# Gated cross-attention and a routed feed-forward on one core: the two additions of a wide tile to the output, each half with a semaphore of its own

## The reference, cut to what matters

```
x = x + tanh(g_xattn) * cross_attention(ctx, layernorm(x))      # 16 x 256 tokens, width 256, 8 heads of 128
n = layernorm(x)
gates = (n @ Wg + bg) / 1.000001
weights, experts = top_k(gates, 2);  weights = softmax(weights)  # 8 experts
for each token:
    x += tanh(g_ffn) * sum over its 2 experts e of
         weight_e * (silu(n @ W1[e] + b1[e]) @ W2[e] + b2[e])    # hidden width 1024
```

## Time and profile before

| | us |
|---|---|
| median of 3 runs (lowest, highest) | 1546.25 (1545.76, 1546.97) |
| the profiled execution | 1545.36 |
| its span | 1543.7 |
| PE busy | 1502.7 |
| additions (L926, 71): time of the instructions on POOL | 119.9 |
| additions: idle time of POOL before them | 207.2 |

### The profile page before, as it was taken

The page is one execution under the profiler, slowest core; times in us unless marked ns, Lnnn a source line. Parts: engine busy times, 40 slices in busy tenths (PEclk is TensorE's granted clock), DMA queues, the critical chain, the costliest instruction groups (busy, mean ns, idle before and its releaser), DMA issues.

```text
span 1543.7 us, 29968 instructions
## 1 busy us (share of the span) xinstructions
PE 1502.7 (97%) x10446; PEld 1384.4 (90%) x10446; DVE 1114.2 (72%) x2692; ACT 949.8 (62%) x2057; POOL 596.2 (39%) x710
## 2 busy tenths in 40 slices
PE   8999999999999999999999999999999999999986
PEld 6889888898888889898888888888999999999976
DVE  7677777777777777777777777777767766666675
ACT  5555655556555655556556555556668777777765
POOL 5332424334342333423334342332444545444442
PEclk9999999999999999999999999999999999999999
DMA  4000100000000000000000000022546645544553
GB/s 164 4 21 8 22 8 22 28 8 22 8 22 7 22 29 8 22 8 22 29 1 29 8 22 8 8 79 67 121 136 192 162 128 137 150 127 127 150 145 82
DMA packets 57823, 91.13 MB, mean 59 GB/s; under 512 B 8617, under 2 KB 44774, under 8 KB 57550
## 3 DMA queue, kind: packets, MB, share of 16 engines
q1 hardware_dynamic: 41710, 70.19, 14.4%
q0 software_dynamic: 15824, 18.98, 6.6%
q10 hardware_dynamic: 144, 0.05, 0.0%
HBM read 70.91 MB, written 18.29 MB: 58 GB/s over the span
## 4 chain that ended last, share of the span: by engine, by line
PE 81%; DVE 9%; DMA 5%; ACT 2%; issue 2%; POOL 1%; ACTq 0%; DVEq 0%; POOLq 0%
PE ring L194 12%; PE ring L195 12%; PE ring L196 12%; PE turn L1269 6%; DMA out_rows<-yo,token 4%; PE ph L196 3%; PE score L194 3%; PE ph L194 3%; PE py L194 3%; PE py L196 3%; PE py L195 3%; PE ph L195 3%; PE score L196 3%; PE score L195 3%; PE proj L195 2%
## 5 line engine op out<-in xcount | busy, mean ns | idle before, releaser
L901 POOL TENSOR_SCALAR probs<-probs,rsum 128x512 f32<-128x512 f32 x256 | 174.2, 692 | 532.4 <-DVE rsum L1589 532.4
L1115 ACT ACTIVATE pt_hi<-turn 128x512 fp32r<-128x512 f32 x256 | 139.2, 595 | 238.5 <-PE turn L1269 238.5
L926 POOL DMA_INDIRECT out_rows<-yo,token x71 | 119.9, 1689 | 207.2 <-DMA out_rows<-yo,token 133.4
L1714 DVE TENSOR_TENSOR ht_lo<-hs,ht_hi 128x512 fp32r<-128x512 f32 x142 | 98.2, 691 | 120.9 <-ACT ht_hi L1082 117.5
L1583 DVE TENSOR_REDUCE smax<-score 128x1 f32<-128x512 f32 x256 | 169.7, 685 | 13.5 <-PE score L196 13.1
L1016 ACT ACTIVATE probs<-score,nbias 128x512 f32<-128x512 f32 x256 | 173.2, 686 | 3.6 <-DVE nbias L1585 3.6
L1073 ACT ACTIVATE hs<-ph,vecs 128x256 f32<-128x256 f32 (+1 forms) x284 | 114.5, 458 | 98.1 <-PE ph L196 90.0
L1824 DVE TENSOR_TENSOR pt_lo<-turn,pt_hi 128x512 fp32r<-128x512 f32 x256 | 164.2, 682 | 8.8 <-ACT pt_hi L1115 8.7
L194 PE MATMUL py<-w_hi,ht_lo 128*128 (+1 forms) x568 | 163.7, 288 | 2.7 <-DVE ht_lo L1714 2.0
L195 PE MATMUL py<-w_lo,ht_hi 128*128 (+1 forms) x568 | 161.6, 285 | 0.9 <-issue 0.9
L196 PE MATMUL py<-w_hi,ht_hi 128*128 (+1 forms) x568 | 161.6, 285 | 0.0
(11 more groups left out here) (248 smaller groups left out, 4707.9 us busy)
## 6 DMA issues: line engine op xcount, KB each, us to landing
w_raw<-in_L_ffn_W SPq DMA_DIRECT2D x45, 1024.0 KB, 8.4
xhat_rows<-rows SPq DMA_DIRECT2D x16, 264.0 KB, 2.2
x_raw<-in_x SPq DMA_DIRECT2D x16, 256.0 KB, 3.2
c_raw<-in_ctx SPq DMA_DIRECT2D x16, 256.0 KB, 3.3
out_rows<-x SPq DMA_DIRECT2D x16, 256.0 KB, 2.7
xg<-xhat_rows,token POOLq DMA_INDIRECT x71, 4.0
out_rows<-yo,token POOLq DMA_INDIRECT x71
v_raw<-in_L_xattn_Wkv SPq DMA_DIRECT2D x2, 512.0 KB, 8.1
```

The costliest lines, as they stand in the source:

```text
L901: last = pool.tensor_scalar(probs[n % 2][:, t, :], probs[n % 2][:, t, :], rsum[:, n % 2, t:t + 1], 1.0, ALU.mult, ALU.mult)
L926: pool.indirect_dma_start(out=A["out"], out_offset=bass.IndirectOffsetOnAxis(ap=token[:, u:u + 1].bitcast(U32), axis=0), in_=yo_of(t)[:, s ...
L1115: act.activation(pt[0][:, 2 * t:2 * t + 2, :], turn[t][:, :].rearrange("p (j i) -> p j i", j=2), ACT.Copy).then_inc(s_pthi, 1)
```

## The change

Each half gets its own semaphore: `s_add` becomes a pair. `added(t, half)` gives how many additions of that half stand before tile t: t for the first halves, and at most 31 for the second ones. A scatter of tile t waits until both halves of all tiles before t have landed, and no more for the other half of its own tile. On POOL both halves of tile t - 1 are issued in iteration t, behind each other and behind the gathers of that iteration; the second half of tile t - 2 no longer stands in it. `finish` waits for the half or halves that it overwrites, by the new counts.

```diff
--- before.py
+++ after.py
@@ -532,7 +532,9 @@
         s_w2hi, s_w2lo = sem("w2_hi"), sem("w2_lo")
         s_px, s_xhi, s_xlo = sem("x_turned"), sem("xt_hi"), sem("xt_lo")
         s_ph, s_silu, s_hhi, s_hlo = sem("hidden"), sem("hidden_act"), sem("ht_hi"), sem("ht_lo")
-        s_l2, s_pyr, s_w, s_yo, s_add = sem("y_pair"), sem("y_read"), sem("w_ready"), sem("y_out"), sem("added")
+        s_l2, s_pyr, s_w, s_yo = sem("y_pair"), sem("y_read"), sem("w_ready"), sem("y_out")
+
+        s_add = sem("added_first"), sem("added_second")
         s_warm = sem("table_warm")
 
         N_HOME_READY = 4
@@ -626,6 +628,10 @@
 
         def turned_of(n):
             return (routing, ph[(FIRST_N + 2) % N_PH])[(n - FIRST_N) % 2]
+
+        def added(t, half):
+
+            return min(t, WIDE) if half else t
 
         def by_step(function, t):
 
@@ -915,18 +921,19 @@
                 ).then_inc(s_gathered(t), 16)
 
             def scatter(t, s):
+
                 u = row_of(t) + s
                 pool.wait_ge(s_yo, u + 1)
-                if u:
-
-                    pool.wait_ge(s_add, 16 * u)
+                if t:
+                    for half in range(SUB):
+                        pool.wait_ge(s_add[half], 16 * added(t, half))
                 else:
                     for i in range(2):
                         pool.wait_ge(s_x2st[i], 16 * (B // 2))
                 pool.indirect_dma_start(
                     out=A["out"], out_offset=bass.IndirectOffsetOnAxis(ap=token[:, u:u + 1].bitcast(U32), axis=0),
                     in_=yo_of(t)[:, s, :], in_offset=None, compute_op=ALU.add,
-                ).then_inc(s_add, 16)
+                ).then_inc(s_add[s], 16)
 
             for c in range(2):
                 cols = slice(TT * c, TT * (c + 1))
@@ -975,21 +982,22 @@
                             gather(later, s)
                 if t == 1:
                     list_tokens(B - 1)
-                    scatter(0, 0)
+                    for s in range(SUB):
+                        scatter(0, s)
                     pool.wait_ge(s_row, 1)
                     pool.wait_ge(s_listed, 16 * TOP * TT * B)
                     pool.indirect_dma_start(
                         out=names[0:LATE_SUB, 0:P], out_offset=None, in_=dram["lists"],
                         in_offset=bass.IndirectOffsetOnAxis(ap=row[0:LATE_SUB, :].bitcast(U32), axis=0),
                     ).then_inc(s_names, 16)
-                if t >= 2 and subs(t - 2) == 2:
-                    scatter(t - 2, 1)
                 if t == 3:
                     for s in range(SUB):
                         gather(EARLY + 1, s)
                 if t > 1:
-                    scatter(t - 1, 0)
-            pool.wait_ge(s_add, 16 * ROWS)
+                    for s in range(subs(t - 1)):
+                        scatter(t - 1, s)
+            for half in range(SUB):
+                pool.wait_ge(s_add[half], 16 * added(N_TILES, half))
 
         @program("scalar")
         def _(act):
@@ -1744,12 +1752,17 @@
                     if t == EARLY:
                         dve.wait_ge(s_b2, 16)
                     bias = b2[:, bass.ds(e * D, D)]
-                if t >= WIDE + N_YO:
-                    dve.wait_ge(s_add, 16 * row_of(t - SUB * N_YO + 1))
+
+
+                if t >= WIDE + SUB * N_YO:
+                    dve.wait_ge(s_add[0], 16 * added(t - SUB * N_YO + 1, 0))
+                elif t >= WIDE + N_YO:
+                    dve.wait_ge(s_add[1], 16 * added(t - SUB * N_YO + 1, 1))
                 elif t >= WIDE:
-                    dve.wait_ge(s_add, 16 * (row_of(t - N_YO) + 1))
+                    dve.wait_ge(s_add[0], 16 * added(t - N_YO + 1, 0))
                 elif t >= N_YO:
-                    dve.wait_ge(s_add, 16 * row_of(t - N_YO + 1))
+                    for half in range(SUB):
+                        dve.wait_ge(s_add[half], 16 * added(t - N_YO + 1, half))
                 n = subs(t)
                 dve.tensor_tensor(yo_of(t), py[t % 2][:, 0:n * D].rearrange("p (s d) -> p s d", s=n),
                                   bias.unsqueeze(1).to_broadcast([P, n, D]), ALU.add).then_inc(s_pyr, 1)
```

## The result

| | us |
|---|---|
| changed kernel, median of 4 runs (lowest, highest) | 1533.53 (1533.44, 1533.60) |
| kernel before, 4 runs beside it | 1546.01 (1545.31, 1546.97) |
| ratio, 95% interval | 0.9919 (0.9902 to 0.9936) |
| profiled execution, its span | 1533.60, 1531.9 |

The kernel is 12.5 us faster.

The account below looks back on a forecast made before the run. PE was taken to bound the kernel (busy 1502.7 of 1543.7 us). Terms 5.90 + 2.16 + 1.84 + 0.47 = 10.4 us took 1545.36 to 1535.0; with 0.9 added, forecast 1535.9 us, range 1534.0 to 1541.5.

Parts of the forecast that it names:

- PE's wait: PE's stop for the copy `flat` before the turned step at 1488.83 would go, giving back 5.90 us.
- the low clock behind it: PE's lower clock level just after its 5.9 us wait would go, giving 2.16 us; bounds 0 to 2.2.
- both waits for gathers: PE's waits at tile 10 (1.44 us) and the first narrow gathers (0.40) would go; 1.8 us, bounds 0 and 1.8.
- The first rival: Paired additions share DMA engines and serialize; only the order helps, moving the linked chain by 7.2 us to 1539.0; chance 0.14.
- the second rival: Loads of W1 become late beside the paired additions; each of the last 7 tiles loses about 1 us, 1543 us; chance 0.07.
- The level: The median of the runs was taken to lie 0.9 us above the profiled execution, turning 1535.0 into 1535.9 us.
- Tiles 0 to 28: Early stretch of the routed part, holding PE's gather wait at tile 10; forecast gain 1.44 us.
- The first narrow gather: PE's wait for the first narrow gathers, in the stretch of tiles 28 to 31; forecast gain 0.40 us.
- The end: Lag of the last addition shrinks from 1.18 us to an issue's 0.71; gain 0.5 us, bounds -1 and 0.5.
- The stop at tile 32: PE's 5.90 us wait plus 2.16 us of lower clock behind it; 8.06 us for tiles 31 to 39.
- the step that I called normal: The second step on PE after the wait, 3.25 us to 1497.80, was taken to carry no clock surcharge.
- PE and DVE set the end: At the kernel's end PE and DVE were taken as the bound, with the queue of additions adding 1.2 us.

Follow-up runs that it names:

- the kernel with the new order alone: Changed kernel with additions one at a time again: a wide tile's second half also waits until its first half landed; 1540.70 us, ratio 0.9986 to the kernel before.
- the later jobs: The changed kernel run again beside the kernel before in two jobs on other chips; 1535.41 us (ratio 0.9931) and 1533.43 us (ratio 0.9932).
- the late part old: Changed kernel up to tile 19, with order and one-at-a-time additions of the kernel before from tile 20 on; 1536.26 us, ratio 0.9939 to the kernel before.
- three tiles overlapped: Old order and one-at-a-time additions as in the kernel before, except that tiles 12 to 14 may overlap their halves; 1540.21 us, ratio 0.9981.
- the kernel with other halves: Kernel before, with narrow tiles using both halves of yo1 first, so tile 32 overwrites a half added one place earlier; 1544.67 us, ratio 1.0016.

## Why the prediction was off

Right by its own steps: PE's wait was followed back to the first half of tile 30, and taking away the lag of the queue took away the 5.9 us, the low clock behind it and both waits for gathers. No copy of W1 waited for its load, the gathers landed as fast as before with additions in flight beside them, and a pair of additions does overlap.

The first rival, the serial pair, is the kernel with the new order alone. The prediction ties the rule that two such transfers serialize, from the Trainium skill, page "DMA: Bandwidth & Descriptors", section "Rules for kernel authors", to the second rival, but it is this one. The measurement decides against it here: about 7 us for a pair instead of 11.7. The rule speaks of disjoint halves of the partitions, while by the code each half of `yo` lies across all 128. The rival's price was wrong as well. It gave the serial pair 7.2 us of gain, 1539.0; the kernel's 1540.70 looks near, but the kernel before took 1542.63 in that job, so the gain was 1.9 us. The chain did not move by one landing as a whole, since PE waited for gathers (3.2 us, and the clock behind them).

Wrong in size, 10.1 us forecast (10.4 by its sum) and 12.5 measured. The step that failed is the sizing, in two parts that make up the 2.4 us between 1535.9 and 1533.5: the sum of the terms, 10.37 against 11.80 in the table above, and the level added to it.

- The level, 1.0 us. I added 0.9 us, by which the profiled execution of before lay under its median. The changed kernel's median lies 0.07 us under its profiled execution. It rests on one execution on either side, and with executions of one kernel several us apart it is chance as far as is known.
- Tiles 0 to 28, 0.5 us. At tile 10 I took PE's idle time, 1.44 us. The interval from the read of tile 7 to that of tile 8, in which this stop lies, shrank by 1.69 (13.45 to 11.76). The rest is in tiles 0 to 3.
- The first narrow gather and the tiles around it, 28 to 31: 0.73 instead of the idle time of 0.40 us.
- The end, 0.6 us. I took the 0.71 us of an issue in the chain as the least lag of the last addition. With nothing ahead of it, it went out 0.28 us after its data (1523.97 to 1524.25). That is 0.43 us, and 0.19 behind it.
- Tiles 31 to 39, 0.3 us. The stop at tile 32 itself was sized right. The turned steps of the changed kernel, to be held against the earlier trace rows, and the last one of each kernel (L1332 is the kernel before):

```profile
1477.46 0.60 PE L1340 MATMUL ph<-ident,flat 128*128 128x128 f32 x4
1480.70 0.60 PE L1340 MATMUL routing<-ident,flat 128*128 128x128 f32 x4
1484.50 0.60 PE L1340 MATMUL ph<-ident,flat 128*128 128x128 f32 x4
1487.75 0.60 PE L1340 MATMUL routing<-ident,flat 128*128 128x128 f32 x4
...
1517.27 0.60 PE L1340 MATMUL ph<-ident,flat 128*128 128x128 f32 x4
```

```profile
1527.99 0.60 PE L1332 MATMUL ph<-ident,flat 128*128 128x128 f32 x4
```

The changed kernel is ahead by 2.07 us at the step in front of the stop (1479.53 against 1477.46), by 8.13 at the one behind it, by 10.05 at the next and the one after that. So the stop with its clock cost 7.98 us, where I had 8.06, and the step that I called normal was. The lead of 10.05 us grows to 10.72 at the last step, in small pieces whose cause was not followed.

Against this, 0.35 us was lost ahead of tile 0, where the code did not change. Each part is about 1 us or less, and the low end of the range left 1.9 us for all of them. That the miss of the range is partly chance shows in the later jobs: gains of 10.8 and 11.0 us, 0.4 to 0.9 above the forecast's.

And one step was incomplete in a way that the time did not show: "at the change to narrow tiles the additions of the last wide tiles are still queued". They are, but some 5 of the 13 us of lag were there at tile 8 and carried for 20 tiles, by a queue whose additions, one at a time, are 6.6 to 7.2 us and 4.5 to 5.2 us apart, some 11.7 together, the period of a tile. Without that part there is no wait: experiments with the late part old or three tiles overlapped show this. I also held that "PE and DVE set the end"; the kernel with other halves shows that removing that one wait gives nothing, so the 8 us belong to the queue and not to the wait.

What is open: why the early additions land late, and why the two gaps add up to the period of a tile for 20 tiles. A load of W1 is issued once per tile, and in tiles 25 and 26 of the kernel before the long gap is the one behind the addition issued within 0.8 us of it (1414.17 beside the load of 1414.89, 1426.11 beside 1426.64). That fits a slow addition beside each load, but no kernel here took the loads away. Nor was the drift of the attention part followed up.

## What to carry to other kernels

A serial queue whose service time per tile is about the tile's period need not recover from a delay: here it carried one for 20 tiles to the first place where the slack is used up, far from where it arose. Look for its lag (data ready to issue) at several tiles, not only at the wait. The wait that the profile names need not be what the queue costs: here another stood right behind it, through the gathers on the same engine, and only an edit to the queue itself gave the time back. Price a stop of PE by the same PE instructions in a kernel with and without it, not by its idle time alone, and not by another engine's reads, which shift against PE. Hold a variant's time against the kernel before in the same job: 1540.7 us looked like most of a forecast that it was not.

## What was not expected of the hardware

Two indirect additions of 128 KB, issued 1.9 to 2.4 us apart, were both done before the next tile's pair in the wide tiles from tile 4 on, and a pair took about 7 us where the trace gives its end. One at a time they are mostly 4.5 to 7.2 us from issue to the next issue, up to 10 in the first tiles. What a stop of PE costs beyond its idle time does not follow from its length: 0.25 us for one of 1.44 us, 1.8 us for one of 2.12 us and 2.1 us for one of 5.90 us, and 1.6 us for 3.5 us in two pieces. The first left the granted clock at 1.00, behind the others it was at the lower level for some us.
